# A four-layer graph network on one core: in the last stage, row weighting and the final norm move from VectorE to ScalarE

## The reference, cut to what matters

```
side = segment_sum(edge_weight[:, None] * x[dst], src, num_segments=100000)
x = layernorm(x + (x + 3 * side) / 4)      # per row of 128
```

## Time and profile before

| | us |
|---|---|
| time before, median of 3 runs | 6070.19 (6068.53 to 6072.99) |
| the profiled execution's own time | 6065.45 |
| its span in the trace | 6063.7 |
| last stage in it, from the first gather (5031.67) | 1032 |

### The profile page before, as it was taken

How to read it: one execution, slowest core, us unless ns; L and a number is a source line. 1 busy time by engine, 2 the same in 40 slices (tenths; PEclk the granted TensorE clock), 3 DMA queues, 4 the chain that set the end, 5 groups by cost and what they waited for, 6 DMA issues and landing times. The chain is left out here.

```text
span 6063.7 us, 102666 instructions
## 1 busy us (share of the span) xinstructions
PE 4372.9 (72%) x25328; PEld 3184.7 (53%) x25328; DVE 4395.3 (72%) x8168; ACT 3147.5 (52%) x6667; POOL 4424.6 (73%) x4339
## 2 busy tenths in 40 slices
PE   1059899998888799999989999888888883422200
PEld 0047788886666677777765555544444442211100
DVE  8966799996888688888865555599999995743300
ACT  0047788886666455555544444378888882110000
POOL 7777677775777777777767777577777766777777
PEclk9999999999999899999999999988888875555555
DMA  5377688885889799999977777634444438943311
GB/s 126 100 142 182 183 253 251 251 251 152 286 284 285 200 261 264 263 262 264 261 199 225 226 226 227 197 105 113 116 116 115 114 105 260 325 140 97 92 40 40
DMA packets 1005237, 1151.72 MB, mean 190 GB/s; under 512 B 184599, under 2 KB 641235, under 8 KB 1004182
## 3 DMA queue, kind: packets, MB, share of 16 engines
q1 hardware_dynamic: 831958, 834.69, 46.4%
q0 software_dynamic: 137984, 247.24, 16.7%
q10 hardware_dynamic: 35136, 68.16, 3.1%
HBM read 688.22 MB, written 523.68 MB: 200 GB/s over the span
## 5 line engine op out<-in xcount | busy, mean ns | idle before, releaser
L1016 PE MATMUL bank<-ident,gat 128*128 128x128 f32 x2352 | 424.2, 310 | 624.4 <-DVE zT L2017 550.2
L1119 PE MATMUL bank<-x1T,W1x 128*128 128x512 f32 x1568 | 763.7, 599 | 23.1 <-ACT x1T L1312 23.1
L1133 PE MATMUL bank<-W2s,hT 128*128 128x128 f32 x6272 | 779.2, 278 | 1.0 <-ACT hT L1396 1.0
L1133 PEld LDWEIGHTS bank<-W2s,hT 128*128 128x128 f32 x6272 | 735.9, 193 | 16.7 <-ACT hT L1396 1.7
L1016 PEld LDWEIGHTS bank<-ident,gat 128*128 128x128 f32 x2352 | 305.4, 161 | 751.1 <-issue 556.4
L1322 ACT ACTIVATE mbuf<-t 128x512 f32<-128x512 f32 x490 | 309.9, 633 | 581.5 <-DVE t L2051 310.1
L1396 ACT ACTIVATE hT<-bank,b1u 128x512 f32<-128x512 f32 x784 | 502.9, 679 | 183.9 <-PE bank L1119 183.6
L1016 PE MATMUL bank<-ident,x 128*128 128x128 f32 x3136 | 482.3, 277 | 90.8 <-DVE x L1982 83.0
L759 POOL DMA_INDIRECT gat<-X,d_x x392 | 396.6, 1012 | 205.5 <-issue 178.6
L796 POOL DMA_INDIRECT VQ<-s_v,s_q x392 | 448.8, 1145 | 119.5 <-issue 114.9
L772 POOL DMA_INDIRECT Y<-x,d_out x392 | 405.6, 1035 | 175.0 <-issue 110.6
(11 more groups left out here) (369 smaller groups left out, 11325.8 us busy)
## 6 DMA issues: line engine op xcount, KB each, us to landing
X<-x SPq DMA_DIRECT2D x588, 256.0 KB, 2.6
fB<-row_s_same SPq DMA_DIRECT2D x392, 256.0 KB, 5.2
Y<-x SPq DMA_DIRECT2D x294, 256.0 KB, 3.9
xT<-in_x_fm SPq DMA_DIRECT2D x196, 256.0 KB
ffB<-rows_last_notlast SPq DMA_DIRECT2D x98, 512.0 KB
out_rows<-Y ACTq DMA_DIRECT2D x28, 1792.0 KB
Z1T<-zT SPq DMA_DIRECT2D x98, 256.0 KB
Z1E<-zE SPq DMA_DIRECT2D x98, 256.0 KB
```

Of the source, the lines that this page charges most:

```text
L1016: mm = pe.transpose(dst[:, t, :], tiles[t], ident[:, :])
L1119: mm = pe.matmul(bH[h][:, :, :], W1x[:, cols], x1T[s][:, :], start=kind != "d", stop=True)
L1133: mm = pe.matmul(bMLP[:, t, :], hT[h][s][:, t * P:(t + 1) * P], W2s[:, h, :], start=False, stop=h == HC - 1, skip_group_check=True)
```

## The change

Weighting the gathered rows and the last multiplication of the norm go to ScalarE, each as four activations of function Copy on 128x128 with a scale that is read per partition from a tile (`wts`, or the reciprocals `lns[3][2]`), instead of one VectorE multiplication of 128x512. VectorE keeps the reciprocal (`fin_scale`), which now hands over through a new count, `scaled`, on a semaphore that the stage before used. VectorE's list becomes `power` g-3, scan g-1, reciprocal g-3, sum g-2; ScalarE's becomes copy, weigh g, norm g-3, square g-2, root g-2.

```diff
@@ semaphores
+            "scaled": ("scale34", EI),
@@ scalar engine, last stage
+            def z_weigh(k):
+                def stage(i, s):
...
+                    at(act, "gathered", s, moved(5 if k == 3 else k, i + 1, s))
+                    for t in range(T):
+                        w = bass.ds((i * SL + s) * T + t, 1)
+                        a = act.activation(gat[s][:, t, 0:P], gat[s][:, t, 0:P], ACT.Copy, scale=wts[:, w])
+                    a.then_inc(S("weighted", s), 1)
...
-            steps(act, EI, (copy_pieces, 0), (square("fin", 3), 2), (std("fin", 3), 2), unrolled=True)
+            def fin_norm(i, s):
...
+                ready(act, "scaled", s, i)
+                fin_free(i, s)
+                dst = held[i][s].rearrange("p (t f) -> p t f", t=T) if i < HB else x4[s]
+                for t in range(T):
+                    a = act.activation(dst[:, t, :], t2[s][:, t, :], ACT.Copy, scale=lns[3][2][s][:, t:t + 1])
+                a.then_inc(S("ln4_out", s), 1)
+            all_slots(act, "agg_turned", EI)
+            steps(act, EI, (copy_pieces, 0), (z_weigh(3), 0), (fin_norm, 3), (square("fin", 3), 2), (std("fin", 3), 2),
+                  unrolled=True)
@@ vector engine, last stage
-            def fin_norm(i, s):
-                dst = [h.rearrange("p (t f) -> p t f", t=T) for h in held[i]] if i < HB else x4s
-                norm("fin", 3, lambda s: t2[s], dst, "ln4_out", fin_free)(i, s)
-            steps(dve, EI, (z_weigh(3), 0), (power("fin", 3), 3), (z_scan(3), 1), (fin_norm, 3), (fin_sum, 2), unrolled=True)
+            def fin_scale(i, s):
...
+                ready(dve, "deviation3", s, i)
+                at(dve, "ln4_out", s, x4i("fin", i))
+                dve.reciprocal(rs[s][:, :], sd[s][:, :]).then_inc(S("scaled", s), 1)
+            steps(dve, EI, (power("fin", 3), 3), (z_scan(3), 1), (fin_scale, 3), (fin_sum, 2), unrolled=True)
```

More of the change, by code:

```diff
@@ L93, in gnn_kernel @@
             "q_out": ("x1T", NI + 2 * EI), "decay": ("relu", NI + 2 * EI), "weight": ("x2T", NI + EI),
-            "att_src": ("z_rows", 2 * EI), "gathered_x": ("gathered_d", 0), "ld_attr": ("st_xd", EI * 16),
+            "att_src": ("z_rows", 2 * EI), "scaled": ("scale34", EI), "gathered_x": ("gathered_d", 0), "ld_attr": ("st_xd", EI * 16),
         }
@@ L1429, in _ @@
             all_slots(act, "st_z2", 2 * EI * 16)
+            def z_weigh(k):
+                def stage(i, s):
+                    c = seq(k, i)
+                    if void(act, i, s, ("weighted", c, 1)):
+                        return
+                    at(act, "gathered", s, moved(5 if k == 3 else k, i + 1, s))
[3 more added lines that the diff above has]
+                    a.then_inc(S("weighted", s), 1)
+                return stage
             def x_src(i, s):
@@ L1484, in copy_pieces, with fin_free @@
                     act.dma_start(out_runs[w, :], src_runs[w, :]).then_inc(S("copied"), 16)
-            steps(act, EI, (copy_pieces, 0), (square("fin", 3), 2), (std("fin", 3), 2), unrolled=True)
+            def fin_free(i, s):
+                if i == HB - 2:
+                    at(act, "st_x3_", s, 2 * EI * 16)
+                elif i == HB:
+                    at(act, "scattered2", s, moved(1, 0, s))
+                elif i > HB:
+                    reuse(act, "scattered", s, i - HB, 64)
+            def fin_norm(i, s):
+                if void(act, i, s, ("ln4_out", x4i("fin", i), 1)):
+                    return
+                ready(act, "scaled", s, i)
[7 more added lines that the diff above has]
+                  unrolled=True)
         @block.vector
@@ L2252, in fin_sum @@
                                          op0=ALU.mult, op1=ALU.add).then_inc(S("fin_sum", s), 1)
[L2254 to L2260, removed]
-            def fin_norm(i, s):
-                dst = [h.rearrange("p (t f) -> p t f", t=T) for h in held[i]] if i < HB else x4s
-                norm("fin", 3, lambda s: t2[s], dst, "ln4_out", fin_free)(i, s)
-            steps(dve, EI, (z_weigh(3), 0), (power("fin", 3), 3), (z_scan(3), 1), (fin_norm, 3), (fin_sum, 2), unrolled=True)
+            def fin_scale(i, s):
+                if void(dve, i, s, ("scaled", i, 1)):
+                    return
+                _, sd, rs, _ = lns[3]
+                ready(dve, "deviation3", s, i)
+                at(dve, "ln4_out", s, x4i("fin", i))
+                dve.reciprocal(rs[s][:, :], sd[s][:, :]).then_inc(S("scaled", s), 1)
+            steps(dve, EI, (power("fin", 3), 3), (z_scan(3), 1), (fin_scale, 3), (fin_sum, 2), unrolled=True)
 def kernel(**inputs):
```

## The result

The changed kernel takes 6038.63 us in the median of 6 runs (6036.94 to 6047.35), beside 6069.76 (6068.53 to 6077.54) for the kernel before in the same set of runs: ratio 0.9949, 95% interval 0.9936 to 0.9962. A second set of 5 runs gave 6046.16 (6044.19 to 6046.91), ratio 0.9962 (0.9949 to 0.9976). So it is 23 to 31 us, or 0.4 to 0.5%, faster. The forecast was 6060 and the range went from 6049 to 6072. The profiled execution took 6038.07 us (span 6036.3), 27.4 less than that of before.

A forecast was written before the change was run, and what follows sets the result against it. POOL's indirect DMAs were taken to bound the last stage. Scatters 7.2 plus gathers 2.5, 9.7 us off the profiled 6065.45, gave 6055.8; with 4.7 us to the median, 6060.5, rounded to 6060; range 6049 to 6072.

The forecast's parts named there:

- Scatters: POOL's scatters in the last stage: those lengthened by VectorE's two-SBUF-operand multiplications become plain, 7.2 us back in full.
- Gathers: POOL's gathers before the first scatter: of 8.0 us of lengthening, 2.5 us come back, DMA queues being 96% occupied.
- Copies: ScalarE's DMA issue of 28 copies: they go out up to one landing earlier, same bytes, worth nothing.
- upper bound: Gathers before the first scatter: at most all 8.0 us plus two waits less their gaps, 11.9 us.
- Latency: Late gather to first scatter: turn starts about 1.3 us after landing, not 2.6; slower ScalarE steps offset it, costed at nothing.
- ScalarE's step: ScalarE's work per group after the change: 4.2 us, bounds 3.1 and 5.0, so it keeps up with POOL.
- All of it comes back: Rival, before the first scatter: POOL sets the pace, DMA only close behind; 19.1 us gained, 6051 us; chance 0.28.
- the two late waits: POOL's idles of 1.68 us ahead of the gather at 5322.07 and 2.84 ahead of the first scatter.
- Another cause: Rival, POOL's lengthened calls: something else, say a DMA ring, lengthens them; nothing changes, 6070 us; chance 0.12.
- ScalarE becomes the bound: Rival, before the first scatter: ScalarE's hand-overs in sequence take 6.2 us per group and POOL stands; 6116 us; chance 0.10.
- From profile to median: Whole kernel: the median of the runs lies 4.7 us above the profiled execution, added to the forecast.

The follow-up runs named there:

- e5: The changed kernel run again without any edit, for a second profile and more runs; median 6046.2 us, ratio to before 0.9962.
- e12: Changed kernel with POOL's scatter five groups behind its gather instead of four and one copy at the start instead of three; 6046.5 us, ratio to before 0.9957.
- e4: Kernel before plus one wait on ScalarE, after its copies of a step, until that step's gather has landed; 6063.7 us, ratio to before 0.9991.
- e9: Changed kernel with four copies instead of three sent ahead of ScalarE's first wait; 6052.1 us, ratio to before 0.9969.
- e7: Changed kernel plus two purposeless VectorE multiplications per group, 128x512, both operands in SBUF; 6059.8 us, ratio to before 0.9988.
- e8: Changed kernel plus two purposeless VectorE multiplications per group, 128x512, one operand from a bank, one from SBUF; 6043.4 us, ratio to before 0.9955.
- e1: Kernel before with VectorE's list reordered to power, scan, norm, sum, weighing last, nothing moved to ScalarE; 6067.6 us, ratio to before 0.9999.

## Why the prediction was wrong

The mechanism was right and two terms of the sum were mis-sized, both in part one. The sum gave 9.7 us for the last stage, and 22.3 were measured. That is 12.6 of the 21.9 us between the forecast (6060.5) and the median; 5.1 more lie ahead of the stage and 4.1 in the step from profile to median, and both are chance: in e5 the stage began 4.0 us later than in the profile of before, not 5.1 earlier.

*Scatters, 7.2 us "come back in full":* right. 7.5 measured, which are the 7.2 and a wait of 0.34 that went too.

*Gathers, "I take 2.5, near the lower end":* the step that failed first; the term was 8.0, not 2.5. All 8.0 us came back: no lengthened gather is left, and part one has only 7.7 us of waits. My reason, that the DMA queues were occupied 96%, took a share near 1 for a rate that can't rise. Over part one it rose from 311 to 327 GB/s, and in the stretch that I had called saturated from 333 to 340. (I also wrote that most of the 96% was the copies'; by the earlier trace rows it is 41.6, less than half.) Landings can still hold POOL up: in e12 it does wait for them, in the middle of part one.

*"Copies: ... same bytes, nothing":* the step that failed second, and it broke the upper bound (11.9 us, while part one gave 14.8). I had seen that ScalarE would now wait for gathers behind its copies, and had looked at the steady run alone, where copies leave a little sooner. At the start they leave later: ScalarE had nothing to wait for in its first two steps, so that its fourth copy of 1792 KB left with the first three and stood in the DMA queues beside the rows of group 1. The waits at the start were 10.0 us before and 4.0 after; e4 takes 5.3 of them away with that wait alone and e9 brings 5.6 back. I had left the two longest waits of POOL in the whole stage, 3.36 and 7.24 us, out of the account, since they are caused by DMA. Part one's sum by what was measured: 8.0 (gathers) + 6.0 (start) + 1.6 (the waits at 5187 and 5322) - 1.2 (the wait at the first scatter, 3.7 for 2.5) = 14.4 of the 14.8.

*Latency, "I cost it at nothing":* nearly right. What fixes the first scatter in both kernels is the norm of group 52, and from the weighing of that group to the first scatter there are 16.4 us before (5322.38 to 5338.81) and 15.1 after (5303.84 to 5318.92). The turn does start sooner after a late landing: in the changed kernel the weighing begins at 5303.84 and the turn at 5305.25,

```profile
5303.84 1.28 ACT L1440 ACTIVATE gat<-gat,wts 128x128 f32<-128x128 f32 x4 [2.90 <-DMA gat<-X,codes_z]
...
5305.25 1.11 PE L1016 MATMUL bank<-ident,gat 128*128 128x128 f32 x4 [5.03 <-ACT gat L1440]
```

1.4 us, where I had 1.3. *ScalarE's step, 4.2 us, bounds 3.1 and 5.0:* 3.9 when nothing is waited for (the timeline's weighings at 5307.76, 5311.67, 5315.58), below POOL's 5.0.

*Rivals.* "All of it comes back" (6051) was nearest. For the stage it stands for 19.1 us, and 22.3 came: it lacked the 6.0 us of the start, which no case of mine had, and it counted 3.9 us for the two late waits, of which 0.2 came back, since the first scatter now waits 3.7 us. "Another cause" is excluded by e7 and e8, "ScalarE becomes the bound" by the waits: between the one at its start and the one at the first scatter the changed kernel has none of over 0.1 us. (That rival's step of 6.2 us adds up to 6.3 with its own terms, and its 6116 to about 6120.) The rule that speaks for VectorE (the Trainium skill, ScalarE: Activation LUTs, "Rules for kernel authors") would have kept the slower kernel: four activations take 1.26 us and the one multiplication 0.69, and the kernel is faster mostly by what the multiplication did to a third engine. *From profile to median* I had added 4.7 us of offset; the medians since lie from 3.9 above to 5.0 below their profiled execution, and the changed kernel's two profiled executions differ by 9 us ahead of the stage. The range should have had some 5 us for that on either side.

## What to carry to other kernels

Where POOL's indirect DMAs set the pace, look at the length of its single calls, not only at who waits for whom: an engine that POOL never waits for can still hold it. Try VectorE instructions with two SBUF operands on ScalarE, even where that makes them slower, or with one operand from a bank (e8 shows only that such an instruction leaves POOL alone, not what it would cost to bring the operand there). Changing the order of VectorE's list is no substitute: in e1 the calls were lengthened by more and the time stayed. And when an engine that also issues DMAs gets a wait, work out when each of those DMAs leaves, at the start of the stage first of all: in the changed kernel one copy's time was worth 6.9 us of the stage (e9), nearly as much as all the lengthened gathers. In the kernel before the same delay brought 1.4 to 3.4 (e4), because other waits and longer calls took its place.

## What the runs showed of the hardware

- POOL's indirect DMA of 128 rows is held by a VectorE instruction with two SBUF operands that is already running. Calls that began 0.10 to 0.40 us after its start were lengthened every time (26 of 26 before, 13 of 13 in e7), by what was left of it at 0.11 us into the call, to within 0.03 us. The longest lengthening of all was 0.54 us. The 14 calls of before that began less than 0.03 us after it kept their length, and it took 0.74 us instead of 0.69. One with a second operand from a bank, equally long, lengthened none of 35 calls (e8).
- The Trainium skill (SBUF — State Buffer, "Who interferes with whom") has the rule on two SBUF inputs, and the trace agrees (e7 and e8, above). Its inference that a `tensor_tensor` spares descriptor generation would leave these calls plain, and they aren't; but each of them also reads its indices from SBUF, and no run tells which part of the call is held.
- One more copy of 1792 KB in the queues holds up 256 KB of gathered rows by 5.6 us (31.1 and 25.5 us to landing), though they are issued from another engine (before and after the change; e9's return of the wait confirms it).
- The profile's DMA share near 1 doesn't say that the rate is at its limit: at 0.95 the engines moved 297 GB/s, at 1.01 333 and 340, at 1.02 343, with more bytes in large copies where the rate was higher.
